# Layer-norm statistics of seven tiles per batch taken by ScalarE's accumulator instead of VectorE's batch-norm instructions

## What is computed

```python
mod = (_silu(c) @ wmod).reshape(4, 6, 1, -1)
sa, ca, ga, sb, cb, gb = (mod[:, i] for i in range(6))    # ga, gb: sign * max(|.|, 0.25)
h = _layernorm(x) * (1 + ca) + sa
x = x + ga * attention(h)          # 16 heads, keys: 4 sinks and a window of the last 128 tokens
h = _layernorm(x) * (1 + cb) + sb
x = x + gb * moe(h)                # top 2 of 16 experts and one shared expert
```

## Time and profile before

| | |
|---|---|
| runs | 349.38 us median of three (348.10 to 352.21) |
| span of the profiled execution | 347.5 us; its own device time is not listed apart, the lowest run is 0.6 us above this span |
| TensorE, VectorE, ScalarE, GpSimd busy over the span | 80%, 67%, 47%, 59% |
| mean granted TensorE clock | 0.913 of full speed |

### The profile page before, as it was taken

The page is one execution under the profiler, slowest core; times in us unless marked ns, Lnnn a source line. Parts: engine busy times, 40 slices in busy tenths (PEclk is TensorE's granted clock), DMA queues, the critical chain, the costliest instruction groups (busy, mean ns, idle before and its releaser), DMA issues.

```text
span 347.5 us, 6287 instructions
## 1 busy us (share of the span) xinstructions
PE 278.8 (80%) x1665; PEld 215.0 (62%) x1666; DVE 231.3 (67%) x899; ACT 162.2 (47%) x518; POOL 205.2 (59%) x254
## 2 busy tenths in 40 slices
PE   4897889998988899989774999898899898886000
PEld 3264457656766576757543989787788787775000
DVE  0477477998889886997885645544345477763990
ACT  3142562278225822556222455454545566654550
POOL 3713116738784777558557356564655578875981
PEclk9996996999899996999988799999999999999555
DMA  7949001133624649702286644454456778869793
GB/s 261 330 132 347 16 2 49 59 100 115 197 80 135 183 127 320 163 30 93 72 228 205 201 138 121 144 177 133 138 160 180 245 210 254 263 188 343 247 360 139
DMA packets 41438, 59.80 MB, mean 172 GB/s; under 512 B 5092, under 2 KB 29880, under 8 KB 41404
## 3 DMA queue, kind: packets, MB, share of 16 engines
q1 hardware_dynamic: 34312, 39.91, 39.4%
q0 software_dynamic: 6528, 17.90, 14.3%
q10 hardware_dynamic: 564, 1.59, 1.4%
HBM read 33.57 MB, written 25.80 MB: 171 GB/s over the span
## 4 chain that ended last, share of the span: by engine, by line
PE 54%; DVE 22%; DMA 7%; issue 7%; ACT 4%; POOL 2%; another core or an unknown queue 1%; SPq 1%; DVEq 0%; POOLq 0%; ACTq 0%
PE bank L1227 16%; PE bank L892 8%; PE bank L1237 8%; PE bank L1085 6%; PE bank L1029 3%; PE bank L1052 3%; DVE bank L1752 3%; PE bank L1105 3%; DMA ht<-in_L_attn_x_dram 2%; PE bank L1067 2%; DVE h_sb L1369 2%; DMA ys<-pt_win,row_i 2%; PE bank L935 1%; PE bank L906 1%; DMA p_win<-slots 1%
## 5 line engine op out<-in xcount | busy, mean ns | idle before, releaser
L648 POOL DMA_INDIRECT ys<-pt_win,row_i x72 | 72.6, 1009 | 51.0 <-ACT pt_win L676 27.5
L1227 PE MATMUL bank<-ht,w_now 128*128 128x128 f32 x576 | 78.3, 280 | 4.4 <-issue 4.4
L593 POOL DMA_INDIRECT slots<-h_sb,slot_i x64 | 63.2, 987 | 30.1 <-issue 15.3
L1227 PEld LDWEIGHTS bank<-ht,w_now 128*128 128x128 f32 x576 | 71.7, 195 | 5.4 <-issue 5.1
L1741 DVE TENSOR_TENSOR act_t<-bank,sg 128x128 f32<-128x128 f32 x72 | 20.9, 290 | 48.5 <-ACT sg L843 33.2
L676 ACT ACTIVATE ht<-bank 128x256 f32<-128x256 f32 x104 | 39.9, 383 | 22.5 <-PE bank L892 15.6
L1237 PE MATMUL bank<-w_dn,act_t 128*128 x144 | 44.8, 393 | 5.4 <-DVE act_t L1741 4.3
L676 ACT ACTIVATE pt_win<-bank 128x256 f32<-128x256 f32 (+1 forms) x88 | 37.2, 423 | 21.7 <-PE bank L1237 9.6
L1085 PE MATMUL bank<-w_route,ht 128*128 128x272 f32 x128 | 41.5, 452 | 5.5 <-ACT ht L676 3.2
L892 PE MATMUL bank<-ident,p_win 128*128 128x128 f32 x198 | 36.1, 278 | 4.9 <-issue 3.2
L843 ACT ACTIVATE sg<-bank 128x128 f32<-128x128 f32 x72 | 20.1, 279 | 42.2 <-PE bank L1227 29.6
(11 more groups left out here) (260 smaller groups left out, 489.2 us busy)
## 6 DMA issues: line engine op xcount, KB each, us to landing
p_win<-slots SPq DMA_DIRECT2D x67, 129.0 KB
slots<-pads SPq DMA_DIRECT2D x28, 129.0 KB
xs<-in_L_attn_x_dram SPq DMA_DIRECT2D x3, 1024.0 KB
wmod_sb<-ys SPq DMA_DIRECT2D x12, 256.0 KB
w_gu<-ys SPq DMA_DIRECT2D x10, 256.0 KB, 2.8
mod_bc<-mod_rows_out SPq DMA_DIRECT2D x4, 512.0 KB, 5.7
w_dn<-in_L_ffn_w_down_dram SPq DMA_DIRECT2D x1, 2048.0 KB
h_sb<-ys SPq DMA_DIRECT2D x8, 256.0 KB
```

The lines of the kernel that those rows point to most:

```text
L593: pool.indirect_dma_start(out=slots, out_offset=bass.IndirectOffsetOnAxis(ap=slot_i[:, k, j:j + 1], axis=0), in_=h_sb[:, j, :], in_offset= ...
L648: pool.indirect_dma_start(out=ys, out_offset=bass.IndirectOffsetOnAxis(ap=row_i[:, col:col + 1], axis=0), in_=y_sb[:, k, :], in_offset=Non ...
L1227: last = mm(bank[2 + k % 2][:, half * P:(half + 1) * P], w_now[:, k % 2, c, half * M:(half + 1) * M], ht[:, k, c, :], start=(c == 0), stop ...
```

## The change

For the seven tiles 0 to 6 of each batch the statistics move. ScalarE runs a new `statistics(b, j)`: a Copy with scale -1/256 whose accumulator gives minus the mean, then, once that has landed, a Square of x plus that bias whose accumulator gives the sum of squares. GpSimd's `rsqrt` adds 256 x epsilon (a new small instruction, once per group) and then raises to -1/2. The missing factor of 16 is multiplied into 1 + cb once, in an instruction that was there already. Tile 7 of each batch stays on VectorE, with its `veps` multiplied by 256. `centre` no longer waits for VectorE. Minus the mean is now ready tile by tile.

```diff
             def rsqrt(b, n):
                 r = normed(b, n)
-                pool.wait_ge(S["ln_veps"], norm_no(b, n))
-                pool.tensor_tensor(rstd[:, r], veps[:, r], minus_half[:, r], ALU.pow).then_inc(S["ln_rstd"], 1)
+                if n == 2:
...
+                else:
+                    pool.wait_ge(S["x_var"], scale_no(b, r.stop))
+                    pool.tensor_scalar(veps[:, r], square_sum[:, r], D * EPS, None, ALU.add).then_inc(S["x_veps"], 1)
+                    pool.wait_ge(S["x_veps"], [m for m in norms if m[0] not in "a2"].index(f"{n}{b}") + 1)
+                    pool.tensor_tensor(rstd[:, r], veps[:, r], minus_half[:, r], ALU.pow).then_inc(S["ln_rstd"], 1)
...
+            def statistics(b, j):
+
+                if j in (0, TPB - 2):
+                    act.wait_ge(ld_x[b], 16 if j == 0 else 32)
+                act.activation(unread[:, 0, :], xcols(b * TPB + j), ACT.Copy, scale=-1.0 / D, accum_out=less_mean[:, j:j + 1])\
+                    .then_inc(S["x_mean"], 1)
+                if b > 0:
+                    act.wait_ge(S["ln_rstd"], norm_no(b - 1, norm_of(b - 1, j)))
+                act.wait_ge(S["x_mean"], scale_no(b, j) + 1)
+                if scale_no(b, j) > 0:
+                    act.wait_ge(S["x_var"], scale_no(b, j))
+                act.activation(unread[:, 1, :], xcols(b * TPB + j), ACT.Square, bias=less_mean[:, j:j + 1],
+                               accum_out=square_sum[:, j:j + 1]).then_inc(S["x_var"], 1)
...
             act.wait_ge(S["const"], N_CONST)
+            statistics(0, 0)
+            statistics(0, 1)
             queries(0)
             second_keys(0, range(CH))
             own_values(0)
-            act.wait_ge(ld_x[0], 16)
             centre(0, 0)
             centre(0, 1)
+            statistics(0, 2)
+            statistics(0, 3)
...
                 centre(b, 3)
+                if b == 0:
+                    statistics(b, 4)
+                    statistics(b, 5)
                 tanh(b, 1)
...
                 if b == 0:
+                    statistics(b, 6)
                     centre(b, 6)
...
                 if b + 1 < B:
+                    statistics(b + 1, 0)
                     centre(b + 1, 0)
+                    statistics(b + 1, 1)
                     centre(b + 1, 1)
                 act_copy(b, 5)
                 h_copy(b, 5)
+                if b + 1 < B:
+                    statistics(b + 1, 2)
+                    statistics(b + 1, 3)
                 tanh(b, 6)
                 act_copy(b, 6)
                 h_copy(b, 6)
+                if b + 1 < B:
+                    statistics(b + 1, 4)
+                    statistics(b + 1, 5)
                 tanh(b, 7)
                 act_copy(b, 7)
                 h_copy(b, 7)
+                if b + 1 < B:
+                    statistics(b + 1, 6)
             tanh(B, 0)
...
-            norm_stats(0, 0, ln)
...
-                if first:
-                    norm_stats(b, 1, ln)
...
-                    norm_stats(b, 3, ln)
                 ranked(b * GPB)
                 placed(b * GPB)
-                if b + 1 < B:
-                    norm_stats(b + 1, 0, ln)
                 at_normalise(b, at)
...
                 activation(b, 7)
-                if b + 1 < B:
-                    norm_stats(b + 1, 1, ln)
```

More of the change, by code:

```diff
@@ L145, in norm_no, with veps_no @@
             return norms.index(f"{n}{b}") + 1
+        by_dve = [n for n in norms if n[0] in "a2"]
+        def veps_no(b, n):
+            return by_dve.index(f"{n}{b}") + 1
         PT_BANK = 6, 6, 4, 6, 5
@@ L195, in bass_adaln_attention_moe @@
         less_mean = sb("less_mean", [P, TPB])
+        square_sum = sb("square_sum", [P, TPB])
+        unread = sb("unread", [P, 2, D])
         scaled = sb("scaled", [P, TPB - 1, D])
@@ L297, in bass_adaln_attention_moe @@
         at_exp at_pt at_pts at_o at_on at_ot at_ots at_out at_x
-        ln_ch ln_veps ln_rstd x_centred x_scaled h_cent h_ready wsd_ready
+        ln_ch ln_veps ln_rstd x_mean x_var x_veps x_centred x_scaled h_cent h_ready wsd_ready
         tr_ps tr_sb gu_ps tanh_ready act_ch act_ready aps_ready act_t_sb y_ps y_added lg_ready top_ch rt_ch masks rank_ps
@@ L549, in last_norm @@
             def last_norm(b):
-                pool.wait_ge(S["ln_veps"], norm_no(b, "a"))
+                pool.wait_ge(S["ln_veps"], veps_no(b, "a"))
                 pool.tensor_tensor(at_rs[:, 1:2], at_rs[:, 0:1], minus_half[:, 0:1], ALU.pow)\
@@ L586, in rsqrt @@
                 r = normed(b, n)
-                pool.wait_ge(S["ln_veps"], norm_no(b, n))
-                pool.tensor_tensor(rstd[:, r], veps[:, r], minus_half[:, r], ALU.pow).then_inc(S["ln_rstd"], 1)
+                if n == 2:
+                    pool.wait_ge(S["ln_veps"], veps_no(b, n))
+                    pool.tensor_tensor(rstd[:, r], veps[:, r], minus_half[:, r], ALU.pow).then_inc(S["ln_rstd"], 1)
[3 more added lines that the diff above has]
+                    pool.wait_ge(S["x_veps"], [m for m in norms if m[0] not in "a2"].index(f"{n}{b}") + 1)
+                    pool.tensor_tensor(rstd[:, r], veps[:, r], minus_half[:, r], ALU.pow).then_inc(S["ln_rstd"], 1)
             def scatter(j):
@@ L729, in at_probs @@
                     copy(pt_sink[:], bank[PT_BANK[g]][0:H * SINKS, 0:P]).then_inc(S["at_pts"], 1)
+            def statistics(b, j):
[10 more added lines that the diff above has]
+                               accum_out=square_sum[:, j:j + 1]).then_inc(S["x_var"], 1)
             def centre(b, j):
-                act.wait_ge(S["ln_veps"], norm_no(b, norm_of(b, j)))
                 if b > 0:
@@ L1349, in norm_stats @@
                 dve.wait_ge(S["ln_ch"], ln.n)
[L1350 to L1354, removed]
+                v.tensor_scalar(veps[:, normed(b, n)], mv[:, normed(b, n), 1], EPS, float(D), ALU.add, ALU.mult)\
                     .then_inc(S["ln_veps"], 1)
@@ L1488, in _ @@
             g.done(v.scalar_tensor_tensor(gates, gsign, -1.0, gabs, ALU.add, ALU.mult))
-            v.tensor_scalar(mod[:, 4 * D:5 * D], mod[:, 4 * D:5 * D], 1.0, None, ALU.add)\
+            v.tensor_scalar(mod[:, 4 * D:5 * D], mod[:, 4 * D:5 * D], 1.0, D ** 0.5, ALU.add, ALU.mult)\
                 .then_inc(S["mod_ready"], 1)
-            dve.wait_ge(ld_x[0], 16)
-            norm_stats(0, 0, ln)
             dve.wait_ge(S["setup_ps"], SMALL_QK)
```

## The result

| | before | changed |
|---|---|---|
| median of 20 runs | 349.91 us (347.06 to 355.03) | 352.94 us (348.44 to 357.07) |
| ratio | | 1.0075, interval 1.0051 to 1.0100 |
| profiled span, clock | 347.5 us, 0.913 | 351.2 us, 0.904 |

The forecast was +2.1 us (+0.6%); measured are +2.6 us by the ratio, which leaves out the runs in the chip's slower state, and +3.0 us by the two medians. In a second sitting, on another chip, the two kernels gave 1.0066 (1.0026 to 1.0107), or +2.3 us.

The account below looks back on a forecast made before the run. It took TensorE to bound the kernel, with ScalarE a link in the seams. +1.05 + 2.05 + 0.3 - 0.45 - 0.84 = +2.1 us on the 349.38 us median gives 351.5 us, range 347 to 357.

Parts of the forecast that it names:

- A tile at 1.1 us: ScalarE's two statistics passes per tile, with 0.1 us for writing out each accumulator: 1.1 us, ends 0.90 and 1.30.
- my lower end of 0.90: ScalarE's cost per tile with no separate accumulator instruction: 0.90 us, which would make the whole change +0.2 us.
- Seam 1, +2.05: Between batches 1 and 2, ScalarE's statistics delay gate_up(1, 6) by 1.2 us, tanh(1, 6) and gate_up(2, 0) by 2.05.
- Seam 0, +1.05: Between batches 0 and 1, ScalarE's statistics of tiles 2 and 3 delay tanh(0, 6) by 1.05 us, which passes through.
- Seam 2, +0.3 against 0.45: Behind batch 2, ScalarE's passes add 0.3 us; TensorE's shorter wait for o_n behind group 0 gains 0.45.
- The waits of 0.47 and 0.84 go: TensorE's seam 2 waits, for o_n and for exponentials behind VectorE's statistics, vanish: gains 0.45 and 0.84, together -1.3 us.
- Nearly everywhere the chain runs through TensorE: Across the kernel, the chain that ended last runs through TensorE; VectorE's batch-norm pieces are on it in seam 2 only.
- Hidden: setup, batch 0, tiles 4 and 5, tile 6, GpSimd: ScalarE passes at these places fit gaps or waits, and GpSimd's additions, some 0.3 us each, stay covered: no cost.
- Rival (a): At tanh(b, 6) and tanh(b, 7) in each seam, unpacked accumulator reads or lower clock cost +5.7 us: 355 us; chance 0.35.
- Rival (b): VectorE sets the pace; in seam 2 its 1.3 + 2.4 us come back, 3.7 us faster: 345.7 us; chance 0.12.
- Rival (c): Square is not in ScalarE's loaded function set: up to 32 table loads, some 30 us, 380 us; chance 0.03.

Follow-up runs that it names:

- second pair: Profiles of the kernel before and the changed kernel, both unchanged, on one chip in one later sitting; ratios to the kernel before 1.0029 and 1.0066.
- first pair: The original profiles of the kernel before and the changed kernel, spans 347.5 and 351.2 us; ratio of the runs 1.0075.
- the relief alone: Kernel before without VectorE's bn_stats and bn_aggr of tiles 0 to 6 in batches 1 to 3; 336.85 us (0.9890), on another chip 349.88 us (0.9984).
- the seams with 1.48: Changed kernel with a second, unread Square per tile, a tile taking 1.48 us; 350.08 us, 1.029 by medians, seams 13.61 us each.
- VectorE put back: Changed kernel with VectorE's bn_stats, bn_aggr and two small instructions put back at the two seam places, results unread; 343.24 us, 1.0103.

## Why the prediction was right

Sign and size came out: +2.1 forecast, +2.6 and +2.3 measured. The mechanism did too: ScalarE's passes stand in front of what both other engines wait for, in the seams. That the sum agrees so well is in part luck. In the second pair the seams cost 4.1 us (forecast 3.4), the heads gave back 2.3 and the other stretches 1.0, so the first stage grew by 0.85 us; 1.45 of the 2.3 us arose in the second stage, which the forecast had only moving along. By its steps:

- **A tile at 1.1 us.** 1.09, from the accumulator written by an instruction of its own that packs to about 0.1. Without the accumulators a tile is 0.91, my lower end of 0.90. The Trainium skill (ScalarE: Activation LUTs, What ACT_TABLE_LOAD costs) has no price for the accumulator, and the estimate from its figures was about 0.9; the trace without accumulators agrees, with 0.91.
- **Seam 1, +2.05.** Measured +1.51 and +1.41. Counted from tanh(1,5), which came 0.97 earlier, `gate_up(1, 6)` was 1.00 late (forecast 1.2), `tanh(1, 6)` 1.80 (2.05), and `gate_up(2, 0)` 1.51 (2.05). Half of what is missing there is VectorE's: from `activation(1, 6)` to `activation(1, 7)` it took 2.85 us instead of 3.12, so it gave back 0.27 that I had passed on whole. The 0.27 lie in one instruction between the two, `h_tile(1, 7)`. Before, VectorE began it while GpSimd was still in `scale`, and it took 0.75 us; now GpSimd is done at 99.78, and it takes 0.49. GpSimd's and VectorE's timelines, before, then changed:

```profile
98.95 1.60 POOL L599 TENSOR_TENSOR scaled<-scaled,mod_bc 128x256 f32<-128x256 f32 x2
100.08 0.75 DVE L1369 SCALAR_TENSOR_TENSOR h_sb<-centred,rstd,mod_bc 128x256 f32<-128x256 f32 x1
```

```profile
98.38 1.40 POOL L612 TENSOR_TENSOR scaled<-scaled,mod_bc 128x256 f32<-128x256 f32 x2
100.89 0.49 DVE L1408 SCALAR_TENSOR_TENSOR h_sb<-centred,rstd,mod_bc 128x256 f32<-128x256 f32 x1
```

- **Seam 0, +1.05.** +0.53 and +0.67: in the first pair `tanh(0, 6)` came 0.72 late, counted from tanh(0,5).
- **Seam 2, +0.3 against 0.45.** -0.28 in the first pair, close to the forecast, and that agreement is luck of the clock: the gaps of 1.63 and 2.28 stood in a stretch of low clock. In the second profile, at a granted clock of 0.90 and more from 132 us on, the seam was 9.53 and the change cost +2.05. In the first pair the low clock set in ahead of the seam after the change, and the stretch there cost +2.66; that it moved is not shown to be the change's doing, since the relief alone has 10.74 us in this stretch once and 8.69 once. What I did wrong there is the use of one seam's gaps without asking at which clock TensorE ran in them; priced like seam 1 it would have been +2.05, and the sum +3.9.
- **The waits of 0.47 and 0.84 go.** Both are gone, but they belonged to one execution: the second profile of the kernel before has neither, so there this part of the sum, -1.3, is nothing. The 0.84 was worth -0.68 in the first pair and nothing in the second, and 0.74 a batch where ScalarE's passes delay VectorE and its own work stays.
- **The chain.** "Nearly everywhere the chain runs through TensorE" was a wrong reading. In the page's chain TensorE has 54% and VectorE 22% of the span, and from 138 to 183 us VectorE has 25 us of it and TensorE 14. In the second profile the five `bn_stats` of batch 1 (66.47 us, 1.64) are on the chain, in seam 0, and those of seam 2 are not. TensorE showed no wait there, which is what the forecast went by; VectorE was closer to setting the pace than I said.
- **Hidden: setup, batch 0, tiles 4 and 5, tile 6, GpSimd.** Right in the profiles. Batch 0 even gained 0.4 to 0.6 us ahead of tanh(0,5), which I had at nothing. No experiment separates that.
- **Not foreseen:** the heads, -0.4 to -1.0 each in five of six, and +1.45 and +1.87 in the untouched second stage. They partly cancel (heads -1.3 and -2.3 in sum), so the total is closer than its parts.

Rival (a), 355 us, is out: it wanted a tile above 1.2 us, and the seams with 1.48 show what that costs. Rival (b), 345.7 us, is out for this change: the kernel got slower, a tile is not under the 0.9 us that it wanted, and VectorE put back costs about 1 us and not 3.7. How much VectorE's relief is worth alone is not settled: 3.7 us once and 0.6 once. Rival (c) is out: no further load. The Trainium skill (ScalarE: Activation LUTs, Table sets) leaves Square unnamed; here it ran 28 times between Exp, Tanh and Copy with none.

## What to carry to other kernels

Moving work from an engine at two thirds to one at a half costs time when the second is the link that both others wait for in turn: read the idle gaps at that link, in microseconds, against the piece that moves, and not the shares. Six pieces of 1.09 us, in seam 1 into gaps of 0.9 to 1.6, made a seam 0.5 to 2 us longer (where the clock had not stretched it before), and once the gaps are full each microsecond counts whole. Before pricing a place by its gaps, look at the granted clock there, and take a second profile of the same kernel where one stretch decides.

## What the runs showed of the hardware

- ScalarE's accumulator output is a separate ACTIVATION_READ_ACCUMULATOR, 0.19 us alone, 0.1 us from its start to that of the next independent instruction, and 0.28 until a pass that needs it starts (97.26 to 97.54).
- VectorE's `bn_stats` of the same 128x256 tile is one instruction of 0.41 us; two ScalarE passes and two reads take 1.09.
- VectorE's `h_tile(b, 7)`, whose two inputs lie in SBUF, takes 0.48 or 0.49 us when GpSimd's `scale` is over, and 0.75 to 0.83 when it starts inside it: in all eight such places in eight profiles (of 24) it ended 0.28 or 0.29 us after the end of `scale`. In the kernel before this is 100.83 and 100.55 us (seam 1, above).
- Two ratios of one program to the kernel before, from two sittings, differed by up to 1.3%. Its profiles differ in where TensorE's clock falls to its low level (up to 3.75 us in one stretch), in a start of ScalarE up to 1.1 us late on finished matmuls, and in a gap of 0.36 to 5.5 us at the start of the second stage.
